# Attention passes of a graph network: eleven further matmuls per group of edges, written to a scratch bank between the steps of the softmax chain

## What is computed

```python
h = (x @ W).reshape(num_nodes, H, F)
al_s = jnp.einsum('nhf,hf->nh', h, a_s)
al_d = jnp.einsum('nhf,hf->nh', h, a_d)
e = jax.nn.leaky_relu(al_s[src] + al_d[dst], 0.2)
emax = jax.ops.segment_max(e, dst, num_segments=num_nodes)
ee = jnp.exp(e - emax[dst])
denom = jax.ops.segment_sum(ee, dst, num_segments=num_nodes)
alpha = ee / (denom[dst] + 1e-16)
out = jax.ops.segment_sum(alpha[:, :, None] * h[src], dst, num_segments=num_nodes)
```

## Time and profile before

| | |
|---|---|
| median of 3 runs | 10322.74 us (10311.37 to 10323.34) |
| the profiled execution | 10342.51 us |
| its span in the trace | 10340.8 us |
| mean granted clock of TensorE over the span | 0.696 |

### The profile page before, as it was taken

How to read it: one execution, slowest core, us unless ns; L and a number is a source line. 1 busy time by engine, 2 the same in 40 slices (tenths; PEclk the granted TensorE clock), 3 DMA queues, 4 the chain that set the end, 5 groups by cost and what they waited for, 6 DMA issues and landing times. The chain is left out here.

```text
span 10340.8 us, 108519 instructions
## 1 busy us (share of the span) xinstructions
PE 5226.6 (51%) x17665; PEld 3177.7 (31%) x17666; DVE 2895.2 (28%) x6396; ACT 2997.3 (29%) x8921; POOL 3419.4 (33%) x3548
## 2 busy tenths in 40 slices
PE   2334444453444444433444442699981444545589
PEld 1212222222222222311222221588870222223334
DVE  8322222233222222422222225011114111112544
ACT  3133333332233233322323331132221333333212
POOL 0344444425444443444443321200015444442000
PEclk9766666666666666666666665799995666666777
DMA  2422222223222221222222112111114222222000
GB/s 86 110 66 58 58 58 58 57 60 90 64 58 58 58 57 49 87 72 63 58 58 55 49 45 99 60 45 60 54 61 120 67 63 68 59 59 65 0 15 18
DMA packets 319707, 632.50 MB, mean 61 GB/s; under 512 B 70272, under 2 KB 200760, under 8 KB 317848
## 3 DMA queue, kind: packets, MB, share of 16 engines
q0 software_dynamic: 173872, 475.54, 16.4%
q1 hardware_dynamic: 138344, 149.65, 4.6%
q10 hardware_dynamic: 7440, 6.82, 0.2%
HBM read 534.38 MB, written 97.76 MB: 61 GB/s over the span
## 5 line engine op out<-in xcount | busy, mean ns | idle before, releaser
L947 POOL DMA_INDIRECT rows<-table,ix x2352 | 2258.6, 960 | 3026.4 <-issue 2998.0
L1150 PE MATMUL acc<-rows,hot 128*128 x5268 | 2055.4, 527 | 1530.8 <-issue 1171.3
L1150 PEld LDWEIGHTS acc<-rows,hot 128*128 128x128 f32 x5268 | 1081.7, 242 | 2448.1 <-issue 2353.8
L1090 ACT ACTIVATE apart<-iota,ndrel 128x128 f32<-128x128 f32 x2640 | 942.5, 397 | 1805.1 <-issue 1531.1
L1067 DVE COPY accs<-acc x228 | 98.7, 433 | 3574.1 <-PE acc L1152 3416.8
L1285 PE MATMUL acc<-rows,hot 128*128 x1756 | 735.1, 564 | 666.7 <-issue 490.0
L1096 ACT ACTIVATE hot<-apart 128x128 f32<-128x128 f32 x2640 | 757.3, 304 | 1023.3 <-PE acc L1150 640.4
L1207 POOL DMA_INDIRECT rows<-emb,ix x784 | 743.3, 948 | 845.3 <-issue 822.3
L1285 PEld LDWEIGHTS acc<-rows,hot 128*128 128x128 f32 x1756 | 391.3, 264 | 991.3 <-issue 967.1
L1052 DVE TENSOR_TENSOR rows<-rows,pw 128x1024 f32<-128x1024 f32 x588 | 671.9, 1214 | 0.0
L1891 PE MATMUL p<-xt,w 128*128 128x256 f32 x2496 | 564.0, 383 | 102.4 <-issue 86.9
(11 more groups left out here) (374 smaller groups left out, 5189.0 us busy)
## 6 DMA issues: line engine op xcount, KB each, us to landing
rows<-table,ix POOLq DMA_INDIRECT x2352
xg<-slots_in SPq DMA_DIRECT2D x79, 256.0 KB
slots_out<-ys SPq DMA_DIRECT2D x78, 256.0 KB
table<-hs SPq DMA_DIRECT2D x147, 130.0 KB
own_row<-table SPq DMA_DIRECT2D x21, 896.0 KB, 11.0
slots_in<-zsp SPq DMA_DIRECT2D x9, 1664.0 KB, 22.0
xin<-in_x POOLq DMA_DIRECT2D x14, 896.0 KB, 5.6
rows<-emb,ix POOLq DMA_INDIRECT x784
```

The costliest lines, as they stand in the source:

```text
L947: pool.indirect_dma_start(rows[:, h * GB + k, 0:RW], None, table, bass.IndirectOffsetOnAxis(ap=ix[:, h, k:k + 1], axis=0)).then_inc(landed ...
L1090: nc.scalar.activation(apart[j][:, :], c.iota[:, 0:P], ACT.Abs, bias=c.ndrel[:, ds(q * 2 + j)]).then_inc(parted, 1)
L1150: nc.tensor.matmul(A, hot[j][:, :], row, start=False, stop=False, skip_group_check=True).then_inc(stepped, 1)
```

## The change

`spare` grows from one column to 128 columns of its PSUM bank. A function `turn_over(n)` issues n matmuls of the 128 x 128 identity with 128 columns of `iota` into it, in float32; nobody reads the result and no semaphore is involved. It is called with 3 behind the transpose to `pS`, with 1 behind those to `prow`, with 3 behind those to `pcar` and with 4 behind those to `pw`, in each group of each pass. The one-column matmul that increments `freed` writes the first column of the wider `spare`.

```diff
-        spare = ps("spare", [P, 1])
+        spare = ps("spare", [P, P])
...
             @block.tensor
             def _(pe):
+                def turn_over(n):
+
+                    for _ in range(n):
+                        nc.tensor.matmul(spare[:, :], c.ident[:, :], c.iota[:, 0:P], start=True, stop=True)
+
...
                         nc.tensor.transpose(pS[:, :], terms[:, :, :].rearrange("p h b -> p (h b)"), c.ident[:, :]
                                             ).then_inc(turned, 1)
+                        turn_over(3)
                         pe.wait_ge(ended, m + 1)
...
                         nc.tensor.transpose(prow[:, 1, :], top[:, 0:1], c.ident[0:HB, 0:HB]).then_inc(rowed, 1)
+                        turn_over(1)
                         pe.wait_ge(rkept, m + 1)
...
                         nc.tensor.transpose(pcar[:, 1:2], back[:, 1:HB + 1], c.ident[0:1, 0:1]).then_inc(carried, 1)
+                        turn_over(3)
                         pe.wait_ge(firsts, m + 1)
...
                         ins.then_inc(paid, 1)
+                        turn_over(4)
                         with pe.Fori(*tiles_of(pe, m)) as n:
...
-                        nc.tensor.matmul(spare[:, :], zero[0:1, 0:P], zero[0:1, 0:1], start=True, stop=True
+                        nc.tensor.matmul(spare[:, 0:1], zero[0:1, 0:P], zero[0:1, 0:1], start=True, stop=True
                                          ).then_inc(freed, 1)
```

## The result

| | before | after |
|---|---|---|
| median | 10321.46 us (10311.37 to 10323.34, 4 runs) | 10481.53 us (10480.84 to 10482.64, 4 runs) |
| span of the profiled execution | 10340.8 us | 10479.2 us |
| mean granted clock over the span | 0.696 | 0.706 |

The ratio is 1.0157, with a 95% interval of 1.014 to 1.0175. The median of the kernel before has one run more than the forecast had (10322.74 from three). The changed kernel was timed twice more, each time beside new runs of the kernel before: 1.0156 (1.0139 to 1.0173) and 1.017 (1.015 to 1.019).

The account below looks back on a forecast made before the run. Each group was taken as bound by its gather and the work left behind it; 0.35 us a group, paid at 0.2 in 81 groups and fully in three, gave +7 us: forecast 10330 us, range 10279 to 10405.

Parts of the forecast that it names:

- Duration and fit: Spares in the softmax chain's gaps: 0.44 us each, three taking 1.32 us, all hidden by VectorE's part, 0 us cost.
- Rival 4: Spares overrun their gaps at `prow` and `pw`, so handovers come late: up to 10405 us; chance 0.12 of over 0.2% slower.
- Sequencer: Four spares behind `pw`, ahead of the loop-bound reads, make a group's first `acc` matmul 0.35 us later.
- the 9.75 to 10.1: Sign of a right forecast: the zeroing `acc` matmul starts 9.75 to 10.1 us after `pS`.
- Clock: TensorE's clock in the softmax chain stays at 0.50 for most groups; no gain counted, at most 0.52 us a group.
- The paid share of a late chain, 0.2: A chain 1 us later against a fixed gather costs 0.2 us in 81 groups, the full microsecond in each pass's last.
- slow steps to about 5 us after the last gather: Sign of a right forecast: slow sequencer steps run from the zeroing `acc` matmul to about 5 us after the last gather.
- Rival 5: Loads and matmuls make sequencer steps behind `pw` slow, up to 1.41 us each: +195 us, 10518; chance 0.08.
- the paced stretch: Part of a group, 1908.2 to 1936 us, where slow sequencer steps space pairs of `acc` slots 9.85 us apart beside gathers.
- a group is set by its gather: A group's time follows its 28 gather issues of 0.95 + 0.30 us and the work left when they end.

Follow-up runs that it names:

- e8_dense: Kernel before plus five wide spare matmuls a group (10 loads, 10 matmuls, 2176 columns), on the chip without slow steps: ratio 0.9918.
- e1_one_column: The changed kernel with its 11 spares cut to one moving column each (22 loads, 22 matmuls a group): ratio 1.0165 against the kernel before.
- e2_wide: The changed kernel with the same 1408 spare columns in four matmuls instead of eleven (8 loads, 8 matmuls): ratio 1.0011 against the kernel before.
- e3_last_four: The changed kernel with only the four spares behind `pw` (8 loads, 8 matmuls a group): ratio 1.0006 against the kernel before.
- g0_before_cut: Kernel before with each gather cut from 128 rows to 16, no spares, on the chip without slow steps: ratio 0.9999.
- l0_late_gather: Kernel before with a group's gathers held until TensorE has summed a first slot of the running group: ratio 1.0394.
- s2_spread: Kernel before with a group's 28 gathers in seven pieces of four, the later five tied to TensorE's slot count: 9483.37 us, ratio 0.9174.

## Why the prediction was wrong

- **Duration and fit: right.** 22 rows of 0.21 to 0.24 us; 1.49 and 1.65 us for three; `prow`, `pcar`, `pw` to 0.01 us where they were. Rival 4 did not happen.
- **Sequencer: the term of 0.35 us did not come, and it was too small to matter.** The zeroing matmul came 9.59 us behind `pS` in the group shown, outside the 9.75 to 10.1 that I had named, and over the 78 groups 0.01 us later than before (9.48 for 9.47). The steps that read the loop bounds stayed fast.
- **Clock: right.** 0.50 in the windowed chain, and from `pS` to `pw` 0.52 on average in both kernels (up to the zeroing matmul, with the last four spares in it, 0.54 for 0.51). The rule of the Trainium skill (TensorE: Matmul & The Clock Gate, Why this matters for your kernels) that asks for continuous work agrees: the change's spares with gaps between them left the chain's clock nearly where it was, and the denser ones of e8_dense raised the clock of the sums.
- **The paid share of a late chain, 0.2: not what failed,** though I had named it as what would. The chain of an ordinary group was not late. Only that of the three first groups was, by 21.0 us in all at the zeroing matmul, and they took 15.9 us more, a share of 0.76 if they paid for nothing else.
- **What failed is a term that the sum put at nothing:** what 22 more loads and matmuls beside the gathers do to the other engines. Every term priced what TensorE does and when its sequencer gets there. None priced when its semaphore increments reach the engines that wait, and I took "adds no wait and no semaphore" to mean that no other engine is touched. The increments of `stepped`, which the change doesn't touch, came over 20 us late in the group shown, and ScalarE's longest wait went from 9.6 to 28.3 us: 146 us where the sum had 7. The sign "slow steps to about 5 us after the last gather" failed with it: the median end of the last slow step was 4.7 us behind the gather's end before, and is 7.5 us ahead of it in the change, as the engines wait from there.
- **Rival 5 had the mechanism half right** and the wrong place: that loads and matmuls use something up is what e1_one_column and e2_wide show, but steps at the loop bounds stayed fast and `hot` was late instead. Its price of 195 us was near the 146 to 160 measured by luck: the nine slow steps that it was worked out from did not occur. What I held against it, that loads and matmuls between two steps cost nothing in the paced stretch, rests on rows with two of each at a time; eight of each more in a group cost nothing to speak of (e2_wide 0.1%, e3_last_four 0.06%), and 22 cost everything. A dose of two says nothing of a dose of 22.
- **The range** stopped at 10405 because rival 5 had 0.08. The paced stretch was an effect that I could describe and not explain; with an unexplained resource beside the place of the change, its bound should have been inside.
- **A reading that fell as well:** that a group is set by its gather holds as it stands only on these chips, where a group takes 64.8 us; on the unpaced chip it takes 41.3 (g0_before_cut). And on these chips the beginning of an unbroken run does no harm, which l0_late_gather's small cost and s2_spread's gain fit.

On the size of such a delay, the Trainium skill (TensorE: Matmul & The Clock Gate, The cost: per-tile semaphore tail) has increments of TensorE serialise at some 26 ns each. Nothing here comes near a sum of such costs: the group above has two increments late by over 20 us.

**What stays open.** What the shared resource is, between the gathers on one side and TensorE's increments and the register steps of three engines on the other, was not found. Why one chip has no trace of it (7695 us for the same kernel) neither; the change itself never ran on that chip, only with cut gathers, so that its full loss vanishes there is argued and not shown. Whether recording the profile takes part is a rival that nothing here tests. That the timed runs agree with the profiled ones to 0.4% does not settle it, for each timed run of the experiments has a span and a granted clock on record too. A count of instructions that matters, where their columns don't, is what such a cause would also show.

## What to carry to other kernels

A filler instruction that waits for nothing and signals nothing can still delay the signals of its engine; test it by its count, with the work held constant, before believing that a gap is free. When an engine waits and the profile says "remote", or names a DMA that has nothing to do with it, look up when the awaited instruction ended: the time between is a late increment, and it is recovered not on the engine that waits but by what crowds it out. Here the crowd is a long run of gather issues. Tying its pieces to TensorE's progress, which broke it into runs of mostly 10 to 15 us with pauses, gained 8.3%, where filling the gaps lost 1.6%.

## What the runs showed of the hardware

- TensorE's semaphore increments can arrive over 20 us late while GpSimd issues indirect gathers (20.5 and 22.9 us in the group shown). 28 loads and matmuls added beside them delay the first groups of a pass, 36 give waits of 12 to 27 us in 70 of 78 groups, and with 44 the wait ends behind the last gather in 64 of 78.
- Register steps of the other engines take 0.7 us, one in 1.40 us, beside a run of gathers. They begin 6.4 us (median) behind its first issue where the sums run beside it and 12 us where the chain does, and end 1.41 us for each gather behind the first issue, with 8 to 28 gathers in the run and with 128 or 16 rows in each.
- The rows moved do not matter (10363.97 us with an eighth of the rows, 10319.25 with all).
- The same kernel takes some 10,320 us (10316 to 10326) on four chips and 7,695 us on a fifth, where no register step is slow. A comparison is worth something only beside the kernel before on the same chip.
